# A @ y2 of a graph layer from seven products of blocks instead of a full product

## The chip, the cores and the metric

The kernel runs on one core of one Trainium2 chip. The metric is the time of one execution on the device in microseconds (us); of several executions the median is taken. The engines of the core are named as the profile names them: PE (TensorE, matrix multiplication; PEld is its loading of weights), DVE (VectorE), ACT (ScalarE), POOL (GpSimd) and SP (SyncE, which here only issues transfers).

## The reference

x is 1250 x 1024, the graph has 41250 edges (with both directions and loops), all weights are 1024 x 1024, all in float32:

```python
def _sage_sum(h, src, dst, Ws, Wn, b):
    h_neigh = jax.ops.segment_sum(h[src], dst, num_segments=N_NODES)
    return h @ Ws + h_neigh @ Wn + b

h = jnp.maximum(_layernorm(x, axis=-1), 0.0)
h = _sage_sum(h, src, dst, Ws1, Wn1, b1)
h = _sage_sum(h, src, dst, Ws2, Wn2, b2)
return x + h
```

The sum over neighbours is a product with A, the 1250 x 1250 matrix of edge counts, so h_neigh @ Wn = A @ (h @ Wn).

## The kernel before

Stage 1 builds A from the edges with one-hot matmuls, normalizes x, and computes y1 = h @ Wn1. Stage 2 computes h1 = h @ Ws1 + A @ y1 + b1, transposed, one feature tile of 128 after the other. Stage 3 is what the change is about.

All of stage 3 has the matrices cut into 2 x 2 blocks. Rows of nodes are padded to 1280, so a block of nodes is 640 = MB (5) tiles of 128 rows; a block of features is 512 = HALF, or KB (4) tiles of 128. First come s2 = h1 @ Ws2 and y2 = h1 @ Wn2, each from seven products of blocks in place of eight (Strassen). The tables say how: LEFT[m] and RIGHT[m] name the one block or the two (with their sum or difference) that product m multiplies, TARGETS[m] the output blocks to which it is added or from which it is subtracted. SEQUENCE is the order of the 14 products ("s" for s2, "y" for y2); the last is ("y", 6). A product runs over KB steps, in each over MB tiles of rows; a number is split into a rounded part (HI) and the remainder (LO), and a tile of a step takes three matmuls of 512 columns. The left sums are made by POOL (L650, from h1T), rounded by ACT (L826) and split by DVE (L1028: sum minus rounded part, both in SBUF). The right sums come ready from DRAM. PE works in eight PSUM banks in turn; `evict` (L1009) adds a finished tile on DVE from its bank to each target, in SBUF. s2 holds x and b2 already when the products begin to be added. The evictions of a product are written down in DVE's program inside the third step of the next product.

Then comes out = s2 + A @ y2, with A whole. y2 is split by column halves: `y2_split_high` on ACT (L805) and `y2_split_low` on DVE (L1015). For every half and every tile t of 128 rows, `neighbours` (L1199) runs 10 source tiles x 2 parts of y2 = 20 matmuls into one bank (L1208); A's entries are small whole numbers and need no split. DVE adds the bank to s2 (L1047, after `dve.wait_ge(tile_done, g + 1)`), and SP writes each tile to the output (L532).

Each engine runs its own program in order and waits on semaphores, so an instruction that waits holds up all behind it on its engine. `bank_free(g)` makes PE wait before the first matmul in a bank until what the bank held is evicted.

Of the kernel before, what the change touches and what calls it, by code (L numbers as in the profile page):

```python
# [4 lines left out]
F32 = mybir.dt.float32  # L5
# [55 lines left out]
            ("y", 2), ("s", 2), ("y", 3), ("y", 6))  # L61
STEPS = len(SEQUENCE) * KB
PARTIALS = len(SEQUENCE) * MB
BANKS2 = (6, 7, 0, 1, 2, 3, 4, 5)
# [47 lines left out]

def evictions():


    seen = set()
    for p, (what, m) in enumerate(SEQUENCE):
# [12 lines left out]
def writes_of(what, row, col, i):  # L130

    seen, found = {"ACT": 0, "DVE": 0}, []
    for p, j, r, c, _, engine in evictions():
        seen[engine] += 1
        if (SEQUENCE[p][0], r, c, j) == (what, row, col, i):
            found.append((p, engine, seen[engine]))
# [96 lines left out]
def gnn_kernel(nc, x, src, dst, ws1, wn1, b1, ws2, wn2, b2, out):  # L233
# [5 lines left out]
    with ctx:  # L239
# [77 lines left out]
        y2_low = at("y2_low", [P, NT, D], F32R, NT * D * 4)  # L317
        y2_high = at("y2_high", [P, 2, NT, HALF], F32R, R0)
# [54 lines left out]
        y2_hi = sem("y2_hi"); y2_lo = sem("y2_lo"); out_ready = sem("out_ready"); out_saved = sem("out_saved")  # L373
# [13 lines left out]
        def wait_step(engine, n):  # L387
# [4 lines left out]
            else:  # L392
                engine.wait_ge(step_done, p * (KB - 1) + k + 1)

# [4 lines left out]
        def _(sp):  # L399
# [128 lines left out]
            for half in range(2):  # L528
                for t in range(NT):
                    r = rows_of(t)  # L530
                    sp.wait_ge(out_ready, half * NT + t + 1)
                    sp.dma_start(out[t * P:t * P + r, half * HALF:(half + 1) * HALF],  # L532
                                 s2[:r, t, half * HALF:(half + 1) * HALF]).then_inc(out_saved, 16)
# [4 lines left out]
        def _(pool):  # L538
# [105 lines left out]
            for n in range(STEPS):  # L644
# [6 lines left out]
                if 3 * KB <= n < 3 * KB + NT:  # L651
                    add_bias(n - 3 * KB)


        @block.scalar
        def _(act):
# [143 lines left out]
            def y2_split_high(half, t):  # L800

                r = rows_of(t)
                act.wait_ge(left_summed, left_sums(10 if half == 0 else len(SEQUENCE) - 1))
                act.wait_ge(dve_evicted, writes_of("y", t // MB, half, t % MB)[-1][2])
                nc.scalar.activation(y2_high[:r, 1 - half, t, :], y2[:r, t, half * HALF:(half + 1) * HALF],  # L805
                                     ACT.Copy).then_inc(y2_hi, 1)

# [3 lines left out]
            for n in range(STEPS):  # L811
# [20 lines left out]
                if 11 * KB <= n < 11 * KB + NT:  # L832
                    y2_split_high(0, n - 11 * KB)
            evict(len(SEQUENCE) - 1, range(MB))
            for t in range(NT):
                y2_split_high(1, t)
# [3 lines left out]
        def _(dve):  # L840
# [152 lines left out]
            done = [0]  # L993

            def evict(p, tiles):
                what = SEQUENCE[p][0]
                for q, i, row, col, op, engine in evictions():
                    if q == p and i in tiles and engine == "DVE":
# [11 lines left out]
                        done[0] += 1  # L1010

            def y2_split_low(half, t):
                r, c = rows_of(t), slice(half * HALF, (half + 1) * HALF)
                dve.wait_ge(y2_hi, half * NT + t + 1)
                nc.vector.tensor_tensor(y2_low[:r, t, c], y2[:r, t, c], y2_high[:r, 1 - half, t, :].bitcast(F32),  # L1015
                                        ALU.subtract).then_inc(y2_lo, 1)

            for n in range(STEPS):
# [17 lines left out]
                if 11 * KB <= n < 11 * KB + NT:  # L1036
                    y2_split_low(0, n - 11 * KB)
            evict(len(SEQUENCE) - 1, range(MB))
            for t in range(NT):
                y2_split_low(1, t)  # L1040
            for half in range(2):
                for t in range(NT):
                    g, r = PARTIALS + half * NT + t, rows_of(t)
                    c = s2[:r, t, half * HALF:(half + 1) * HALF]
                    dve.wait_ge(dve_evicted, done[0])
                    dve.wait_ge(tile_done, g + 1)  # L1046
                    nc.vector.tensor_tensor(c, c, PS[:r, BANKS2[g % 8], :], ALU.add).then_inc(out_ready, 1)  # L1047


        @block.tensor  # L1050
        def _(pe):
# [116 lines left out]
            def bank_free(g):  # L1168
# [4 lines left out]
                elif g - 8 < PARTIALS:  # L1173
                    pe.wait_ge(act_evicted, evicted("ACT", g - 8))
                    pe.wait_ge(dve_evicted, evicted("DVE", g - 8))
                else:
                    pe.wait_ge(out_ready, g - 8 - PARTIALS + 1)

# [20 lines left out]
            def neighbours(half, t, dt):  # L1199
                g = PARTIALS + half * NT + t  # L1200
                bank_free(g)
                for s in range(NT):
                    r = rows_of(s)
                    if t == 0:
                        pe.wait_ge(y2_lo, half * NT + s + 1)
                    for part in (HI, LO):
                        y = y2_high[:r, 1 - half, s, :] if part == HI else y2_low[:r, s, half * HALF:(half + 1) * HALF]
                        ins = nc.tensor.matmul(PS[:rows_of(t), BANKS2[g % 8], :],  # L1208
                                               AT[:r, s, t * P:t * P + rows_of(t)].bitcast(dt), y.bitcast(dt),
                                               start=s == 0 and part == HI, stop=s == NT - 1 and part == LO)  # L1210
                ins.then_inc(tile_done, 1)

            for want, dt in ((0, F32R), (1, F32)):
                with pe.If(redo == want):
# [4 lines left out]
                    for half in range(2):  # L1219
                        for t in range(NT):  # L1220
# [19 lines left out]
```

## Time and profile before

| | |
|---|---|
| median of 3 executions | 660.74 us (658.27 to 661.71) |
| the profiled execution, its own time | 660.24 us |
| its span, first to last instruction | 658.4 us |
| PE busy in the span | 637.4 us (97%) |
| DVE / ACT / POOL busy | 280.3 / 175.7 / 212.4 us |
| PE from the start of s2 and y2 to their end | 372.7 to 563.1 us |
| PE in A @ y2 | 563.1 to 655.0 us |

The profile is of one execution. Matmuls overlap, so the record of one (389 ns) is longer than the time that PE moves on in; that is the length of a stretch divided by its matmuls. On other engines too a record is a little longer than the distance between two instructions in a queue.

### The profile page before, as it was taken

Reading aid. Unit: us, or ns where it says so; the run is one execution under the profiler, and the core shown is the slowest. Engines: PE = TensorE matmul, PEld = TensorE weight load, DVE = VectorE, ACT = ScalarE, POOL = GpSimd, SP = SyncE. Lnnn points to the kernel's source line nnn. Section 1 sums busy time; section 2 is a strip of 40 time slices with the busy share of each in tenths; the row PEclk is TensorE's granted clock in tenths of the full one; section 3 lists DMA queues with packets and bytes.
Section 4 is the critical chain, followed back from the end, with each engine's and each line's share of the span. In section 5 each row is a group of like instructions: output and inputs, shape, how many; then the busy total and the mean of one; then the engine's idle time right before and its main releaser. Section 6 shows DMA issues by size and latency. Waiting matters only on the chain.

```text
span 658.4 us, 8500 instructions
## 1 busy us (share of the span) xinstructions
PE 637.4 (97%) x3280; PEld 555.4 (84%) x3280; DVE 280.3 (43%) x386; ACT 175.7 (27%) x292; POOL 212.4 (32%) x201
## 2 busy tenths in 40 slices
PE   3799999999899999999999999999999999999997
PEld 2688778887799999999999988888888888887885
DVE  2653799783111211120122383325287987611111
ACT  5444343222213313323233121311334433100000
POOL 5432335000247656775680157103214013000000
PEclk9899999999999999999999999999999999999999
DMA  8622330001446766566755766455422243011111
GB/s 276 216 40 56 85 112 33 33 33 62 137 135 196 258 222 232 199 223 202 259 216 176 246 223 231 157 159 160 127 81 69 76 160 96 33 54 59 61 48 62
DMA packets 62724, 90.61 MB, mean 138 GB/s; under 512 B 16545, under 2 KB 34987, under 8 KB 62678
## 3 DMA queue, kind: packets, MB, share of 16 engines
q1 hardware_dynamic: 42342, 76.08, 34.6%
q10 hardware_dynamic: 20336, 13.91, 6.8%
q8 instruction: 30, 0.49, 0.3%
q14 instruction: 16, 0.13, 0.1%
HBM read 58.49 MB, written 31.48 MB: 137 GB/s over the span
## 4 chain that ended last, share of the span: by engine, by line
PE 62%; DMA 1%; DVE 0%; ACT 0%; POOL 0%; issue 0%; SPq 0%; DVEq 0%
PE PS L1192 29%; PE PS L1208 14%; PE PS L1155 10%; PE PS L1163 9%; DMA quarters<-ws_in 1%; DVE W_st L979 0%; POOL prep_sum L617 0%; ACT W_st L728 0%; DVE s L1047 0%; ACT prep L779 0%; SPq L487 0%; DVEq L1046 0%
## 5 line engine op out<-in xcount | busy, mean ns | idle before, releaser
L1192 PE MATMUL PS<-right,left 128*128 128x512 f32 x840 | 190.6, 389 | 0.0
L1192 PEld LDWEIGHTS PS<-right,left 128*128 128x128 f32 x840 | 157.8, 188 | 32.6
L1067 PE MATMUL PS<-W,HT 128*128 128x512 f32 (+1 forms) x480 | 123.0, 406 | 2.5 <-issue 2.4
L1155 PE MATMUL PS<-HT,W_st 128*128 128x416 f32 (+1 forms) x576 | 110.4, 352 | 2.4 <-issue 1.7
L1155 PEld LDWEIGHTS PS<-HT,W_st 128*128 128x128 f32 x576 | 107.9, 188 | 4.0 <-issue 3.1
L1067 PEld LDWEIGHTS PS<-W,HT 128*128 128x128 f32 (+1 forms) x480 | 87.8, 190 | 22.0 <-issue 2.8
L1163 PE MATMUL PS<-AT,y_st 128*128 128x416 f32 (+2 forms) x480 | 92.1, 351 | 0.0
L1163 PEld LDWEIGHTS PS<-AT,y_st 128*128 128x128 f32 (+1 forms) x480 | 90.0, 188 | 0.7
L650 POOL TENSOR_TENSOR left_sum<-h1T 128x640 f32<-128x640 f32 x24 | 41.9, 1746 | 149.9 <-PE PS L1192 120.0
L617 POOL TENSOR_TENSOR prep_sum<-quarters 128x512 f32<-128x512 f32 x40 | 51.6, 1293 | 102.8 <-PE PS L1067 62.8
L1208 PE MATMUL PS<-y_high,AT 128*128 128x512 f32 (+1 forms) x200 | 78.4, 392 | 0.0
L1208 PE MATMUL PS<-y_low,AT 128*128 128x512 f32 (+1 forms) x200 | 78.4, 392 | 0.0
L622 POOL TENSOR_TENSOR prep<-prep_sum,prep 128x512 fp32r<-128x512 f32 x40 | 60.7, 1520 | 25.9 <-ACT prep L779 25.9
L979 DVE TENSOR_TENSOR W_st<-W_st_raw,W_st 128x1024 fp32r<-128x1024 f32 x8 | 14.4, 1798 | 85.2 <-ACT W_st L728 85.2
L1208 PEld LDWEIGHTS PS<-y_low,AT 128*128 128x128 f32 (+1 forms) x200 | 37.2, 186 | 8.8
L1047 DVE TENSOR_TENSOR s<-s,PS 128x512 f32<-128x512 f32 (+1 forms) x20 | 13.7, 687 | 72.0 <-PE PS L1208 72.0
L1208 PEld LDWEIGHTS PS<-y_high,AT 128*128 128x128 f32 (+1 forms) x200 | 37.1, 185 | 8.7
L982 DVE TENSOR_TENSOR y_st<-y_st_raw,y_st 128x1152 fp32r<-128x1152 f32 x8 | 10.9, 1358 | 77.7 <-ACT y_st L765 77.7
L779 ACT ACTIVATE prep<-prep_sum 128x512 fp32r<-128x512 f32 x40 | 23.6, 624 | 64.8 <-POOL prep_sum L617 35.7
L1009 DVE TENSOR_TENSOR s<-s,PS 128x512 f32<-128x512 f32 (+1 forms) x60 | 37.2, 681 | 6.5 <-PE PS L1192 4.5
L924 DVE TENSOR_TENSOR hot_n<-iota_n,pair_key 128x1600 f16<-128x1600 f16 x40 | 39.4, 985 | 0.0
L922 DVE TENSOR_TENSOR hot_m<-iota_m,pair_m 128x1280 f16<-128x1280 f16 x40 | 33.0, 826 | 9.3 <-PE PS L1059 9.2
(79 smaller groups left out, 452.1 us busy)
## 6 DMA issues: line engine op xcount, KB each, us to landing
sums_dram<-prep SPq DMA_DIRECT2D x40, 512.0 KB, 2.9
right<-sums_dram SPq DMA_DIRECT2D x40, 512.0 KB, 3.5
y_dram<-y_out ACTq DMA_DIRECT2D x18, 256.0 KB, 2.1
y_st_raw<-y_dram ACTq DMA_DIRECT2D x8, 576.0 KB
s<-x_in SPq DMA_DIRECT2D x18, 256.0 KB
out<-s SPq DMA_DIRECT2D x18, 256.0 KB
W_raw<-wn_in SPq DMA_DIRECT2D x16, 256.0 KB, 4.0
xin<-x_in SPq DMA_DIRECT2D x8, 512.0 KB, 12.2
```

Of the source, the lines that this page charges most:

```text
L617: nc.gpsimd.tensor_tensor(prep_sum[:, i % PREP, LO, :], quarters[:, QUARTERS.index(a), :], quarters[:, QUARTERS.index(b), :], op).then_inc ...
L622: nc.gpsimd.tensor_tensor(prep[:, i % PREP, LO, :], prep_sum[:, i % PREP, LO, :], prep[:, i % PREP, HI, :].bitcast(F32), ALU.subtract).the ...
L650: nc.gpsimd.tensor_tensor(left_sum[:, k, LO, :], h1_block(*a, k), h1_block(*b, k), op).then_inc(left_summed, 1)
L779: nc.scalar.activation(prep[:, i % PREP, HI, :], prep_sum[:, i % PREP, LO, :], ACT.Copy).then_inc(prep_hi, 1)
L922: nc.vector.tensor_tensor(hot_m[:, u % HOT, :, :, :], iota_m[:, :, :].unsqueeze(1).to_broadcast([P, ROW, P, 2]), pair_m[:, u, :, :].unsque ...
L924: nc.vector.tensor_tensor(hot_n[:, u % HOT, :, :, :], iota_n[:, :, :].unsqueeze(1).to_broadcast([P, ROW, NCOL, 2]), pair_key[:, u, :, :].u ...
L1009: nc.vector.tensor_tensor(c, c, PS[:r, BANKS2[g % 8], :], op).then_inc(dve_evicted, 1)
L1067: ins = nc.tensor.matmul(PS[:r, bank, :], HT[:, a, k, t * P:t * P + r], W[:, k, b, :], start=first and m == 0, stop=last and m == 2)
L1155: ins = nc.tensor.matmul(PS[:, banks[c], 0:w_], W_st[:, a, k, :], HT[:, b, k, o_:o_ + w_], start=k == 0 and m == 0, stop=False)
L1163: ins = nc.tensor.matmul(PS[:, banks[c], 0:w_], y_st[:r, part, s, :].bitcast(dt), AT[:r, s, o_:o_ + w_].bitcast(dt), start=False, stop=s = ...
L1192: ins = nc.tensor.matmul(PS[:, BANKS2[g % 8], :], left[:, k, a, i * P:(i + 1) * P], right[:, KB - 1 - k, b, :], start=k == 0 and j == 0, s ...
L1208: ins = nc.tensor.matmul(PS[:rows_of(t), BANKS2[g % 8], :], AT[:r, s, t * P:t * P + rows_of(t)].bitcast(dt), y.bitcast(dt), start=s == 0 a ...
```

## The change

A @ y2 is now also made from seven products of blocks, in the order NEIGHBOURS = (2, 4, 5, 3, 1, 7, 6) of the same tables, with A's blocks on the left (640 x 640, MB steps of 128) and y2's on the right. Every product is added by DVE's `evict` to the one or two blocks of s2 that TARGETS names. A product has MB steps x MB tiles x 2 parts of y2 = 50 matmuls; the seventh runs tile by tile instead of step by step.

- Left: where LEFT has two blocks (products 2, 5, 1, 7, 6), POOL adds or subtracts them, one 128 x 640 slice per step, into a stage of 4 slots (`a_left_sum`), and SP copies each slice by a transfer into a ring of 8 (`a_left`). 25 sums, 25 transfers.
- Right: where RIGHT has two blocks (products 4, 3, 1, 7, 6), POOL sums a 128 x 512 slice of y2 for the step (`a_right_sum_of`), 25 sums. Every step's slice, sum or single block, is rounded by ACT and split by DVE, 35 times each, into a ring of 5 slots, one per step. A slot is free when PE has finished the same step of the product before.
- The rings lie in the room of h1T. `y2_split_high`, `y2_split_low` and the separate final addition are gone. The output tiles are written when their last eviction is done.

The core of the diff (`wait_a_step(engine, q)` waits until PE has finished step q of this stage):

```diff
+            def a_left_sum(li):
+                q = a_left_steps()[li]
+                a, b, op = LEFT[NEIGHBOURS[q // MB]]
+                if li >= ASTAGE:
+                    pool.wait_ge(a_left_in[(li - ASTAGE) % ALEFT], 16 * ((li - ASTAGE) // ALEFT + 1))
+                nc.gpsimd.tensor_tensor(a_stage[:, li % ASTAGE, :], a_block(*a, q % MB), a_block(*b, q % MB), op).then_inc(a_left_summed, 1)
+            def a_right_sum_of(q):
+                (ra, ca), (rb, cb), op = RIGHT[NEIGHBOURS[q // MB]]
+                wait_a_step(pool, q - MB)
+                pool.wait_ge(dve_evicted, max(written("y", ra, ca, q % MB), written("y", rb, cb, q % MB)))
+                nc.gpsimd.tensor_tensor(a_right_sum[:, q % MB, LO, :], result("y", ra, ca, q % MB), result("y", rb, cb, q % MB),
+                                        op).then_inc(a_right_summed, 1)
+            lefts = 0
+            for q in range(ASTEPS):
+                while lefts < len(a_left_steps()) and (a_left_steps()[lefts] <= q + MB or lefts < MB):
+                    a_left_sum(lefts)
+                    lefts += 1
+                if a_right_is_sum(q // MB):
+                    a_right_sum_of(q)
...
-            for t in range(NT):
-                y2_split_high(1, t)
+            for q in range(ASTEPS):
+                m = NEIGHBOURS[q // MB]
+                if a_right_is_sum(q // MB):
+                    act.wait_ge(a_right_summed, a_right_sums(q) + 1)
+                    whole = a_right_sum[:, q % MB, LO, :]
...
+                nc.scalar.activation(a_right[:, q % MB, HI, :], whole, ACT.Copy).then_inc(a_right_hi, 1)
...
+            last = len(SEQUENCE) - 1
+            for q in range(ASTEPS):
+                p, k = divmod(q, MB)
+                if k == MB - 2 and p:
+                    evict(last + p, range(2))
+                dve.wait_ge(a_right_hi, q + 1)
...
+                nc.vector.tensor_tensor(a_right[:, k, LO, :], whole, a_right[:, k, HI, :].bitcast(F32),
+                                        ALU.subtract).then_inc(a_right_lo, 1)
+                if k == MB - 2 and p:
+                    evict(last + p, range(2, MB))
+                if q == MB - 1:
+                    evict(last, range(MB))
+            evict(last + len(NEIGHBOURS), range(MB))
...
+                def two_products(k, i):
                     for part in (HI, LO):
...
+                        ins = nc.tensor.matmul(PS[:, BANKS2[(PARTIALS + p * MB + i) % 8], :], a_factor(p, k, i).bitcast(dt),
+                                               a_right[:, k, part, :].bitcast(dt),
+                                               start=k == 0 and part == HI, stop=k == MB - 1 and part == LO)
```

In what follows a line of the instruction order is the line of the kernel, the operation, what it writes and reads, its shape, and xN for N in a row.

PE, from the end of the block products to the end of the program. `right`, `left` are the factors of s2 and y2; before, the last rows of 400 that alternate:

```order
L1208 MATMUL PS<-y_high,AT 98x512
L1208 MATMUL PS<-y_low,AT 98x512
L1208 MATMUL PS<-y_high,AT 98x512
L1208 MATMUL PS<-y_low,AT 98x512
L1214 UNCONDITIONAL_BRANCH
```

and now:

```order
1882 L1258 MATMUL PS<-right,left 128x512 x840
1883 L1282 MATMUL PS<-a_right,a_left 128x512 x50
1884 L1282 MATMUL PS<-a_right,AT 128x512 x50
1885 L1282 MATMUL PS<-a_right,a_left 128x512 x50
1886 L1282 MATMUL PS<-a_right,AT 128x512 x50
1887 L1282 MATMUL PS<-a_right,a_left 128x512 x150
1888 L1308 UNCONDITIONAL_BRANCH
```

Seven products of 50 matmuls stand where 400 matmuls stood; five of them take sums of A's blocks from the ring.

POOL, after its last sum of h1's blocks (16 of them in a row close its work before; then its program ends):

```order
162 L640 TENSOR_TENSOR s_92<-s_92,b_sb 128x512 x9
163 L640 TENSOR_TENSOR s_92<-s_92,b_sb 98x512
164 L650 TENSOR_TENSOR left_sum<-h1T 128x640 x16
165 L239 UNCONDITIONAL_BRANCH
```

and now (`a_stage<-AT` is an A sum, `a_right_sum<-y_93` a sum of y2's blocks; this pattern goes on to row 203):

```order
164 L699 TENSOR_TENSOR left_sum<-h1T 128x640 x16
165 L708 TENSOR_TENSOR a_stage<-AT 128x640 x6
166 L714 TENSOR_TENSOR a_right_sum<-y_93 128x512
167 L708 TENSOR_TENSOR a_stage<-AT 128x640
168 L714 TENSOR_TENSOR a_right_sum<-y_93 128x512
169 L708 TENSOR_TENSOR a_stage<-AT 128x640
170 L714 TENSOR_TENSOR a_right_sum<-y_93 128x512
171 L708 TENSOR_TENSOR a_stage<-AT 128x640
```

50 instructions are added behind the end of its program; from the sixth on, each A sum stands directly ahead of a sum of y2's blocks.

DVE, from the middle of the last block product to the end of the program, before (`y_93` is y2, `s_92` is s2; L1009 evicts a bank, L1015 splits y2, L1047 is the final addition):

```order
830 L1009 TENSOR_TENSOR y_93<-y_93,PS 128x512 x6
831 L1028 TENSOR_TENSOR left<-left_sum,left 128x640
832 L1009 TENSOR_TENSOR y_93<-y_93,PS 128x512 x5
833 L1015 TENSOR_TENSOR y_low<-y_93,y_high 128x512 x9
834 L1015 TENSOR_TENSOR y_low<-y_93,y_high 98x512
835 L1047 TENSOR_TENSOR s_92<-s_92,PS 128x512 x9
836 L1047 TENSOR_TENSOR s_92<-s_92,PS 98x512
```

and now, in the fourth to sixth product of A @ y2 (L1077 evicts, L1109 splits):

```order
833 L1109 TENSOR_TENSOR a_right<-a_right_sum,a_right 128x512 x3
834 L1077 TENSOR_TENSOR s_92<-s_92,PS 128x512 x4
835 L1109 TENSOR_TENSOR a_right<-a_right_sum,a_right 128x512
836 L1077 TENSOR_TENSOR s_92<-s_92,PS 128x512 x6
837 L1109 TENSOR_TENSOR a_right<-a_right_sum,a_right 128x512 x4
838 L1077 TENSOR_TENSOR s_92<-s_92,PS 128x512 x4
839 L1109 TENSOR_TENSOR a_right<-a_right_sum,a_right 128x512
```

Splits and evictions alternate: the first two tiles of a product (4 evictions) stand behind the splits of the next product's first three steps.

## Rows read from the trace of the kernel before

**Rows 1.** The chain that ended last: start us, us, what.

```profile
372.72 190.43 PE PS L1192 x840
563.14 91.83 PE PS L1208 x400
655.07 0.69 DVE s L1047
```

**Rows 2.** Busy time by stretch: PE, PEld, DVE, ACT, POOL, clock, DMA share, GB/s.

```profile
563.00:586.00 23.00, 23.00 (x102) 18.89 (x101) 9.71 (x16) 1.76 (x3) 0.00 (x0) 1.00 0.12 46
609.00:632.00 23.00, 23.00 (x102) 18.85 (x101) 3.44 (x5) 0.00 (x0) 0.00 (x0) 1.00 0.15 55
```

**Rows 3.** The page's groups, DVE: busy us, mean ns | idle before, releaser.

```profile
L1047 DVE TENSOR_TENSOR s<-s,PS 128x512 f32<-128x512 f32 (+1 forms) x20 | 13.7, 687 | 72.0 <-PE PS L1208 72.0
```

**Rows 4.** The instructions of L650 on POOL: ns min/median/max, first and last start.

```profile
L650 POOL TENSOR_TENSOR left_sum<-h1T x24: 1567/1593/2290, 376.3 to 549.6; 128x640 f32<-128x640 f32 x24
```

**Rows 5.** Order of time, POOL with full queue: start us, us, instruction, idle before.

```profile
262.61 1.28 POOL L617 TENSOR_TENSOR prep_sum<-quarters 128x512 f32<-128x512 f32 x1 [5.12 <-DMA quarters<-wn_in]
263.86 1.29 POOL L622 TENSOR_TENSOR prep<-prep_sum,prep 128x512 fp32r<-128x512 f32 x1
...
400.03 1.57 POOL L650 TENSOR_TENSOR left_sum<-h1T 128x640 f32<-128x640 f32 x1 [1.83 <-PE PS L1192]
401.56 13.09 POOL L640 TENSOR_TENSOR s<-s,b_sb 128x512 f32<-128x512 f32 x10
```

**Rows 6.** Order of time, DVE and POOL near the end of the block products.

```profile
542.80 0.81 DVE L1028 TENSOR_TENSOR left<-left_sum,left 128x640 fp32r<-128x640 f32 x1
542.83 2.21 POOL L650 TENSOR_TENSOR left_sum<-h1T 128x640 f32<-128x640 f32 x1 [1.83 <-PE PS L1192]
543.53 2.05 DVE L1015 TENSOR_TENSOR y_low<-y,y_high 128x512 fp32r<-128x512 f32 x1
...
545.84 0.83 DVE L1028 TENSOR_TENSOR left<-left_sum,left 128x640 fp32r<-128x640 f32 x1 [0.26 <-ACT left L826]
546.23 1.87 POOL L650 TENSOR_TENSOR left_sum<-h1T 128x640 f32<-128x640 f32 x1 [1.19 <-PE PS L1192]
```

**Rows 7.** Order of time, evictions on DVE across a POOL sum.

```profile
536.45 3.67 DVE L1009 TENSOR_TENSOR s<-s,PS 128x512 f32<-128x512 f32 x6
...
539.43 1.57 POOL L650 TENSOR_TENSOR left_sum<-h1T 128x640 f32<-128x640 f32 x1 [28.67 <-PE PS L1192]
```

**Rows 8.** The instructions of L805 on ACT and L1015 on DVE.

```profile
L805 ACT ACTIVATE y_high<-y x20: 614/616/636, 515.4 to 564.1; 128x512 fp32r<-128x512 f32 x18, 98x512 fp32r<-98x512 f32 x2
...
L1015 DVE TENSOR_TENSOR y_low<-y,y_high x20: 681/689/2059, 516.8 to 569.4; 128x512 fp32r<-128x512 f32 x18, 98x512 fp32r<-98x512 f32 x2
```

**Rows 9.** Order of time, the last matmul.

```profile
654.57 0.40 PE L1208 MATMUL PS<-y_low,AT 98*98 98x512 f32 x1
```

**Rows 10.** Order of time, PE released by DVE.

```profile
245.23 1.94 DVE L979 TENSOR_TENSOR W_st<-W_st_raw,W_st 128x1024 fp32r<-128x1024 f32 x1 [14.71 <-ACT W_st L728]
...
247.32 0.81 PE L1155 MATMUL PS<-HT,W_st 128*128 128x416 f32 x3 [0.68 <-DVE W_st L979]
```

**Rows 11.** PE's pauses near the start in order of time, and stretches as in rows 2.

```profile
13.46 2.90 PE L1067 MATMUL PS<-W,HT 128*128 128x512 f32 x6 [2.42 <-issue]
...
22.28 1.10 PE L1093 MATMUL PS<-ident,hbuf 128*128 128x128 f32 x8 [3.58 <-ACT hbuf L685]
...
15.00:20.00 5.00, 3.70 (x18) 2.71 (x16) 1.79 (x6) 2.06 (x3) 0.16 (x1) 1.00 1.03 371
20.00:25.00 5.00, 2.72 (x13) 2.34 (x14) 5.00 (x9) 2.27 (x2) 4.92 (x4) 0.82 0.88 274
25.00:30.00 5.00, 5.00 (x38) 3.80 (x37) 1.95 (x6) 1.75 (x2) 2.25 (x4) 0.84 0.42 143
```

**Rows 12.** The page's DMA issues: count, KB each, us to landing.

```profile
right<-sums_dram SPq DMA_DIRECT2D x40, 512.0 KB, 3.5
```

More of the change, by code:

```diff
@@ L110, in prepared, with a_left_is_sum, a_left_steps, a_right_is_sum @@
     return [i for i in range(NSUMS) if 1 + i * PARTS // NSUMS == part]
+def a_left_is_sum(p):
+    return len(LEFT[NEIGHBOURS[p]]) == 3
+def a_left_steps():
+    return [q for q in range(ASTEPS) if a_left_is_sum(q // MB)]
+def a_right_is_sum(p):
+    return len(RIGHT[NEIGHBOURS[p]]) == 3
+def a_right_sums(q):
+    return sum(a_right_is_sum(i // MB) for i in range(q))
 def evictions():
     seen = set()
-    for p, (what, m) in enumerate(SEQUENCE):
+    for p, (what, m) in enumerate(SEQUENCE + tuple(("s", m) for m in NEIGHBOURS)):
         blocks = [(what, row, col) for row, col, _ in TARGETS[m]]
@@ L134, in writes_of @@
         seen[engine] += 1
-        if (SEQUENCE[p][0], r, c, j) == (what, row, col, i):
+        if (SEQUENCE[p][0] if p < len(SEQUENCE) else "s", r, c, j) == (what, row, col, i):
             found.append((p, engine, seen[engine]))
@@ L831, in _ @@
                     evict(p - 1, range(2, MB))
[L832 to L835, printed above, removed]
-                y2_split_high(1, t)
+            for q in range(ASTEPS):
[3 more added lines that the diff above has]
+                    whole = a_right_sum[:, q % MB, LO, :]
+                else:
+                    (row, col), = RIGHT[m]
+                    wait_a_step(act, q - MB)
+                    act.wait_ge(dve_evicted, written("y", row, col, q % MB))
+                    whole = result("y", row, col, q % MB)
+                nc.scalar.activation(a_right[:, q % MB, HI, :], whole, ACT.Copy).then_inc(a_right_hi, 1)
         @block.vector
@@ L1035, in _ @@
                     evict(p - 1, range(2, MB))
[L1036 to L1047, printed above, removed]
+            last = len(SEQUENCE) - 1
[4 more added lines that the diff above has]
+                dve.wait_ge(a_right_hi, q + 1)
+                if a_right_is_sum(p):
+                    whole = a_right_sum[:, k, LO, :]
+                else:
+                    (row, col), = RIGHT[NEIGHBOURS[p]]
+                    whole = result("y", row, col, k)
+                nc.vector.tensor_tensor(a_right[:, k, LO, :], whole, a_right[:, k, HI, :].bitcast(F32),
[5 more added lines that the diff above has]
+            evict(last + len(NEIGHBOURS), range(MB))
         @block.tensor
@@ L1197, in partial_products, with a_factor @@
                         ins.then_inc(step_done, 1)
[L1199 to L1205, printed above, removed]
-                    for part in (HI, LO):
[L1207 to L1211, printed above, removed]
+            def a_factor(p, k, i):
+                if a_left_is_sum(p):
+                    return a_left[:, a_left_steps().index(p * MB + k) % ALEFT, i * P:(i + 1) * P]
+                (row, col), = LEFT[NEIGHBOURS[p]]
+                return AT[:, col * MB + k, (row * MB + i) * P:(row * MB + i + 1) * P]
@@ L1218, in _ @@
                         partial_products(p)
[L1219 to L1221 removed]
+                    for p in range(len(NEIGHBOURS)):
+                        neighbour_products(p, dt)
 def kernel(x, src, dst, L0_gnn_Ws1, L0_gnn_Wn1, L0_gnn_b1, L0_gnn_Ws2, L0_gnn_Wn2, L0_gnn_b2):
```

86 lines of the change are left out of this document (61 added, 25 removed).

## The prediction

> **What bounds the kernel now.** I read the chain of waits first. From 372.72 us to the end it names only the matrix engine: 840 matmuls of the block products in 190.43 us, then 400 matmuls of A @ y2 in 91.83 us, then one addition of 0.69 us that starts 655.07 us into the span [rows 1]. That is 0.2296 us for a matmul of A @ y2 (91.83 / 400) and 0.2267 us before it (190.43 / 840). The table by stage says how alone the engine is there: in 609 to 632 us PE is busy 23.00 of 23.00 us, DVE 3.44, ACT and POOL nothing; only in the first stretch, 563 to 586, is DVE still splitting, 9.71 us [rows 2]. DVE's 20 additions of this stage waited 72.0 us in all for PE [rows 3]. So PE sets the end, each matmul taken away is worth 0.2296 us, and the question is what the emptied engines can carry.
>
> **What goes.** 400 matmuls become 7 products x 5 steps x 5 tiles x 2 parts = 350. Matmuls keep their shape, so 50 x 0.2296 = 11.5 us go if PE never waits. (At 0.2267 us it would be 12.5; I keep 0.2296, since these products too take one part of y2 after the other.) Also gone are the 20 splits of y2, ten beside the last block products and ten beside the first tiles. They lay under a busy PE and are worth nothing, except that DVE reaches the new work sooner.
>
> **What comes.** A product now lasts only 25 x 2 x 0.2296 = 11.5 us, a step 2.3 us. Against that:
> DVE, in each of the five products with two targets: 10 evictions and 5 splits at 0.61 us each (3.67 us for six in a row [rows 7], splits alike) = 9.2 us. It fits.
> ACT: 5 roundings of 0.62 us [rows 8] = 3.1 us. It fits.
> POOL: a sum of A blocks has the form of the sums of h1 blocks, 128x640, of 1567 to 1593 ns when undisturbed [rows 4]; behind one that started at 400.03 the next began at 401.56, so 1.53 us in a queue. A 128x512 sum of y2 blocks has the form of those that start at 262.61 and 263.86, 1.25 us apart [rows 5]. The ring of A sums is filled a product ahead, one A sum before each y2 sum, so while the fourth, fifth and sixth product run, POOL owes 5 x (1.53 + 1.25) = 13.9 us for each 11.5 us of PE.
> The 25 transfers of an A sum are 320 KB; the nearest row lands 512 KB in 3.5 us [rows 12]. They have 8 places and run most of a product ahead: nothing.
>
> **POOL and DVE exclude each other here.** A split on DVE that began at 543.53 lasted 2.05 us instead of the usual 0.69 [rows 8]. POOL's sum of 542.83 ended at 545.04, the split 0.54 us later. In turn that sum took 2.21 us, not 1.57: DVE's split of 542.80 ended at 543.61, and 545.04 - 1.57 is 543.47. The pair at 545.84 and 546.23 reads the same (POOL 1.87) [rows 6]. So either engine waits for the other; a split between two queued POOL sums holds POOL up by 0.54 - 0.14 + 0.04 (end of a record against its neighbour) = about 0.45 us. Evictions do not: six ran from 536.45 in 3.67 us across a POOL sum of 1.57 [rows 7]; one operand of theirs is in PSUM. The Trainium skill, SBUF — State Buffer, "Who interferes with whom", says why: a DVE instruction with two SBUF inputs and a GpSimd instruction that reads SBUF exclude each other wholly, one with a single SBUF input does not. The trace agrees in both halves. By that rule the 35 splits and 50 sums of the new stage can never overlap.
>
> **Who waits for it.** On DVE's queue a product's first two tiles are evicted only after three splits of the next product. PE needs the first of these banks at that product's fourth tile, 3 x 0.46 = 1.4 us after its start. So PE waits when the third split is late.
> Second product: POOL may sum y2 for k = 0 when PE has finished the first step, 565.5. Sum 1.29 to 566.8, A sum to 568.3, split 0.45, then sum, A sum, 0.45, sum: 573.2. ACT to 573.9; the next A sum holds DVE to 574.8, split 0.55, two evictions 1.2, 0.2 until PE restarts: 576.7. (The restart: a DVE result at 245.23 + 1.94 = 247.17, the matmul at 247.32 [rows 10].) PE wanted the bank at 563.0 + 11.5 + 1.4 = 575.9: it waits 0.8, and 0.75 more for the next tile (two evictions and a restart, less a tile's work). The third product needs no y2 sums: no wait.
> From the fourth product's first y2 sum POOL is never idle. It may start when the third product's first step is done: 563.0 + 11 x 2.296 + 1.6 waited + 0.2 = 590.1. Up to the sixth product's third y2 sum it owes 13 x 1.25 + 12 x 1.53 + about 12 x 0.45 = 40.0 us: 630.1. ACT to 630.8, the A sum in progress to 631.7, split 0.55, two evictions, restart: 633.7. That is when PE gets its fourth bank of the sixth product, and all waits before it are contained in it: a product in which POOL makes ten sums takes 5 x (1.53 + 1.25 + 0.45) = 16.1 us, so PE waits 4.6 in the fifth and as much in the sixth, and by difference 2.0 in the fourth. Then 1.2 us to the next tile, whose 21 pairs of matmuls to the product's end take 21 x 0.459 = 9.6: 644.5. The last product runs tile by tile and wants all five splits within its first 5 pairs. The last y2 sum can start only now; at 645.3 behind a split, to 646.6, ACT 647.2, split 647.9, restart: PE waits at its fifth pair (due 646.4) till 648.1, 1.7 us. 21 pairs are left, 9.6 us: 657.7. The final addition starts 0.24 us after the last matmul's slot (654.57 + 0.23 against 655.07 [rows 9]) plus 0.69: 658.6.
> Before, it ended at 655.76. The sum is +2.9 us: 11.5 saved, 14.4 waited (1.6, 2.0, 4.6, 4.6, 1.7). What follows, the landing of a last tile of the same size, is unchanged. On the profiled execution's 660.24 that gives 663.1 us, which stands 0.4% above the median of 660.74.
>
> **Rivals.**
> (a) PE is fed throughout: 660.24 - 11.5 = 648.8. For it: PE did not wait from 372.72 us to its end, and POOL, ACT stood idle. Against: POOL's 13.9 us to PE's 11.5 needs no subtle mechanism.
> (b) The queue of POOL binds, but a split costs it nothing (because the sums of A run further ahead, or splits fall into gaps). Then the fifth and sixth product wait 13.9 - 11.5 = 2.4 each and the last one 1.3 (1.7 less the 0.4 behind a split): 11.5 - 6.1 = 5.4 us gained, 654.8. Against it stand the four records of [rows 6].
> (c) Slower, plainly: POOL's sums on A are 5% longer, or splits hold POOL up by 0.55 each. From 590.1 on POOL is the chain, so 34.6 us x 5% = 1.7, or 12 x 0.1 = 1.2, goes fully into the end; with both, and with the second product's wait and the last product's grown alike, some 4 us: 667.1. It decides as soon as POOL has no idle left, which by the sum is the whole time from 590.1.
> (d) The waits lower PE's clock. After 3.58 us without matmuls, at 22.28, the granted clock of 20 to 25 us is 0.82, that of 15 to 20 us 1.00: part of it at 1.2 instead of 2.4 GHz. After the pause of 2.42 us before 13.46 it stayed at 1.00 [rows 11]. The waits of the fifth and sixth product are 3.9 us in one piece. Such a pause cost (1 - 0.82) x 5 + (1 - 0.84) x 5 = 1.7 us of PE's work there; but in these products PE has 4.6 us of waiting in which it makes that up, so only a loss near the end counts: +1.7 twice at most, 666.5. The Trainium skill, TensorE: Matmul & The Clock Gate, "Why this matters for your kernels", holds that a pause between bursts of matmuls can send the engine back to its lower clock; it speaks against this change.
>
> **How the numbers follow.** The forecast 0.70, with its own range 661 to 666: whether a split meets a POOL sum at its start or its end moves a wait by up to 1.5 us, and several of these add. (a) 0.04, (b) 0.10, (c) 0.10, (d) 0.06. A measurement of this kernel tells 0.5% from no change: under 657.4 is faster, over 664.0 slower. The forecast gives slower 0.28 and the same 0.40 of its 0.70, with a little to faster; (a) and (b) are faster, (c) and (d) slower. Together: faster 0.15, same 0.42, slower 0.43. For 8 in 10 the range leaves out (a) and most of (b), and takes in the bounds of (c) and (d): 656.5 to 667.5.
>
> **What would show it.** In the profile after: 350 matmuls of the new line, PE with idle time before them of some 14 us, ended by DVE's evictions, two waits near 4 us in the fifth and sixth product; POOL busy nearly without a gap from 590 to 645 us; splits whose mean is well over 0.69 us and A sums over 1.57. If the splits are at 0.69 us and the POOL sums at 1.6, (b) is right; if PE shows no idle, (a); if the clock of 615 to 650 us is under 1.00, part of (d). I am wrong if POOL's sums are shorter than the rows of before, or if PE's waits are ended by ACT or a transfer.

## The result, and the profile after

Six executions of each kernel, on the same chips in turn: 666.4 us median (664.0 to 667.6) against 660.2 (658.3 to 661.7). The ratio is 1.0089 with a 95% interval of 1.0069 to 1.0109. The change makes the kernel slower by 0.9%. The prediction was 663.1, slower by 0.4%: its direction was right and its range held the time, but the slowdown came out more than twice as large. The profiled execution took 667.12 us, of which 665.3 are the span. Here and below, executions more than 1.5% above the fastest of their kernel are left out of every comparison.

What answers to [rows 1 and 3], in order of time on PE (start us, us, instruction, idle before it and who ended it), from the last block product to the end:

```profile
559.72 2.88 PE L1258 MATMUL PS<-right,left 128*128 128x512 f32 x12
562.44 11.96 PE L1282 MATMUL PS<-a_right,a_left 128*128 128x512 f32 x50
574.24 1.52 PE L1282 MATMUL PS<-a_right,AT 128*128 128x512 f32 x6
576.55 0.70 PE L1282 MATMUL PS<-a_right,AT 128*128 128x512 f32 x2 [0.78 <-DVE s L1077]
577.74 9.78 PE L1282 MATMUL PS<-a_right,AT 128*128 128x512 f32 x42 [0.49 <-DVE s L1077]
587.36 11.50 PE L1282 MATMUL PS<-a_right,a_left 128*128 128x512 f32 x50
598.69 1.52 PE L1282 MATMUL PS<-a_right,AT 128*128 128x512 f32 x6
601.49 0.70 PE L1282 MATMUL PS<-a_right,AT 128*128 128x512 f32 x2 [1.27 <-DVE s L1077]
602.69 11.42 PE L1282 MATMUL PS<-a_right,AT 128*128 128x512 f32 x42 [0.50 <-DVE s L1077]
613.95 1.52 PE L1282 MATMUL PS<-a_right,a_left 128*128 128x512 f32 x6
617.57 0.70 PE L1282 MATMUL PS<-a_right,a_left 128*128 128x512 f32 x2 [2.10 <-DVE s L1077]
618.77 11.16 PE L1282 MATMUL PS<-a_right,a_left 128*128 128x512 f32 x48 [0.49 <-DVE s L1077]
633.65 0.70 PE L1282 MATMUL PS<-a_right,a_left 128*128 128x512 f32 x2 [3.72 <-DVE s L1077]
634.84 12.52 PE L1282 MATMUL PS<-a_right,a_left 128*128 128x512 f32 x48 [0.49 <-DVE s L1077]
648.07 0.70 PE L1282 MATMUL PS<-a_right,a_left 128*128 128x512 f32 x2 [0.71 <-DVE a_right L1109]
650.46 11.39 PE L1282 MATMUL PS<-a_right,a_left 128*128 128x512 f32 x42 [1.69 <-DVE a_right L1109]
```

Where PE had no idle there are now ten waits. Eight stand before the fourth and fifth tile of the second, fourth, fifth and sixth product and are ended by an eviction (L1077); two stand in the seventh product and are ended by a split (L1109). A record of a matmul (0.39 us) is longer than its slot (0.227), so each wait is 0.16 us longer than the idle shown. Together PE waited 13.8 us, where the prediction had 14.4. The waits are thus not what was missing in the sum.

The groups of POOL and DVE in the page after (busy us, mean ns | idle before):

```profile
L714 POOL TENSOR_TENSOR a_right_sum<-y 128x512 f32<-128x512 f32 x25 | 40.4, 1619 | 15.2 <-PE PS L1282 15.1
L708 POOL TENSOR_TENSOR a_stage<-AT 128x640 f32<-128x640 f32 x25 | 42.1, 1693 | 0.0
...
L1109 DVE TENSOR_TENSOR a_right<-a_right_sum,a_right 128x512 fp32r<-128x512 f32 x25 | 30.1, 1208 | 17.0 <-ACT a_right L906 16.4
```

A sum of y2 blocks takes 1.62 us where 1.29 was the undisturbed record [rows 5], a split 1.21 where 0.69 was the median [rows 8]. That is what the exclusion of [rows 6] would do; the experiments test it.

And by stretch, as in [rows 2] (PE, PEld, DVE, ACT, POOL, granted clock, DMA share, GB/s):

```profile
600.00:617.00 17.00, 13.70 (x51) 10.40 (x50) 13.15 (x18) 3.16 (x5) 17.00 (x11) 0.90 0.25 96
617.00:633.00 16.00, 11.86 (x50) 9.23 (x50) 12.17 (x16) 3.16 (x5) 16.00 (x11) 1.00 0.27 102
633.00:640.00 7.00, 5.86 (x19) 4.49 (x20) 7.00 (x12) 1.90 (x3) 5.62 (x5) 0.76 0.14 50
640.00:650.00 10.00, 8.07 (x35) 6.06 (x33) 7.43 (x10) 2.53 (x4) 5.59 (x4) 1.00 0.98 360
650.00:662.00 12.00, 11.39 (x42) 8.93 (x42) 3.12 (x6) 0.00 (x0) 0.00 (x0) 0.86 0.37 138
```

POOL is busy 17.00 of 17.00 and 16.00 of 16.00 us: it is the bound there. The clock is below 1.00 in three stretches, each behind a wait; behind the wait of 2.10 us at 617.57 it stayed at 1.00. The 42 matmuls from 577.74 took 9.78 us; those from 602.69 took 11.42, those from 650.46 11.39.

### The profile page after: what moved, and what is told of

Same layout as the page of the kernel before. It is cut to its first block and busy times, and to the rows that moved or that the text cites. A ratio compares the mean times of both kernels' runs of the same rounds, so it can differ in the third digit from the quotient of the medians.

```text
span 665.3 us, 8676 instructions
## 1 busy us (share of the span) xinstructions
PE 632.3 (95%) x3230; PEld 548.4 (82%) x3230; DVE 328.5 (49%) x441; ACT 186.0 (28%) x307; POOL 296.8 (45%) x251
## 5 line engine op out<-in xcount | busy, mean ns | idle before, releaser
L1135 PEld LDWEIGHTS PS<-W,HT 128*128 128x128 f32 (+1 forms) x480 | 86.4, 187 | 23.8 <-issue 2.8
L1077 DVE TENSOR_TENSOR s<-s,PS 128x512 f32<-128x512 f32 (+1 forms) x120 | 74.4, 677 | 17.5 <-PE PS L1282 7.9
L1282 PE MATMUL PS<-a_right,a_left 128*128 128x512 f32 x250 | 62.1, 406 | 9.3 <-DVE s L1077 6.8
L1282 PEld LDWEIGHTS PS<-a_right,a_left 128*128 128x128 f32 x250 | 48.5, 196 | 22.4 <-issue 12.3
L714 POOL TENSOR_TENSOR a_right_sum<-y 128x512 f32<-128x512 f32 x25 | 40.4, 1619 | 15.2 <-PE PS L1282 15.1
L708 POOL TENSOR_TENSOR a_stage<-AT 128x640 f32<-128x640 f32 x25 | 42.1, 1693 | 0.0
L1109 DVE TENSOR_TENSOR a_right<-a_right_sum,a_right 128x512 fp32r<-128x512 f32 x25 | 30.1, 1208 | 17.0 <-ACT a_right L906 16.4
```

The costliest lines, as they stand in the source:

```text
L708: nc.gpsimd.tensor_tensor(a_stage[:, li % ASTAGE, :], a_block(*a, q % MB), a_block(*b, q % MB), op).then_inc(a_left_summed, 1)
L714: nc.gpsimd.tensor_tensor(a_right_sum[:, q % MB, LO, :], result("y", ra, ca, q % MB), result("y", rb, cb, q % MB), op).then_inc(a_right_su ...
L1077: nc.vector.tensor_tensor(c, c, PS[:r, BANKS2[g % 8], :], op).then_inc(dve_evicted, 1)
L1135: ins = nc.tensor.matmul(PS[:r, bank, :], HT[:, a, k, t * P:t * P + r], W[:, k, b, :], start=first and m == 0, stop=last and m == 2)
L1282: ins = nc.tensor.matmul(PS[:, BANKS2[(PARTIALS + p * MB + i) % 8], :], a_factor(p, k, i).bitcast(dt), a_right[:, k, part, :].bitcast(dt), ...
```

## Experiments

Three questions were open. Is it POOL's queue that binds, or only the place of the evictions in DVE's queue? Does the exclusion of POOL and DVE cost what the sum says, or is it DVE's added work? And what does the clock cost? A time below is a median; a ratio, with its 95% interval, is to the kernel before, run in turn on the same chip.

**Evictions ahead of the third split.** One condition in DVE's program:

```diff
-                if k == MB - 2 and p:
+                if k == MB - 3 and p:
                     evict(last + p, range(2))
                 dve.wait_ge(a_right_hi, q + 1)
```

> DVE evicts the first two tiles of a product before the third split of the next one instead of behind it. Theory POOL (from the fourth product on, POOL's queue of sums, held up further by splits, is the chain): the waits at the fourth tile shrink in the second and fourth product, but the fifth and sixth still wait some 2.7 + 0.8 us each and new waits of about 1 us appear at a product's last step; the end moves by 1 to 2 us only, 664 to 665.5 us against 666.4. Rival ORDER (the place of the evictions in DVE's queue is what costs): nearly all 10 us of waits for evictions go, about 656 us.

663.8 us, ratio 1.0049 (1.0012 to 1.0085). That is a little less than the 664 to 665.5 expected. The waits of the second and fourth product for a bank are gone, those of the fifth and sixth are not, and PE waits at last steps for splits instead:

```profile
607.15 2.57 PE L1282 MATMUL PS<-a_right,AT 128*128 128x512 f32 x10 [0.59 <-DVE a_right L1109]
609.55 1.52 PE L1282 MATMUL PS<-a_right,a_left 128*128 128x512 f32 x6
613.61 13.59 PE L1282 MATMUL PS<-a_right,a_left 128*128 128x512 f32 x50 [2.54 <-DVE s L1077]
629.68 0.70 PE L1282 MATMUL PS<-a_right,a_left 128*128 128x512 f32 x2 [2.47 <-DVE s L1077]
```

If DVE's order were the cause, 10 us would have gone; 2 to 3 went. The order passes most of POOL's lateness on, it is not its source.

**Without the sums of A's blocks.** SP's transfer takes a slice of A itself, and POOL's `a_left_sum` is not called:

```diff
-                sp.wait_ge(a_left_summed, li + 1)
-                sp.dma_start(a_left[:, li % ALEFT, :].bitcast(F32), a_stage[:, li % ASTAGE, :]).then_inc(a_left_in[li % ALEFT], 16)
+                sp.dma_start(a_left[:, li % ALEFT, :].bitcast(F32), a_block(*LEFT[NEIGHBOURS[q // MB]][0], q % MB)).then_inc(a_left_in[li % ALEFT], 16)
```

> Leaves out part of the computation: the 25 sums of A's blocks on POOL; the ring takes a slice of one block of A instead, by the same transfers. Theory POOL: POOL owes 6.2 us per product instead of 13.9, so no wait for evictions is left but one of 0.5 us in the second product, the last product still waits some 1.7 us, the last eviction ends 9.5 us earlier than in the kernel before (655.8 - 9.5 = 646.3 us into the span), about 651 us in all. Rival ORDER: POOL's sums were not the cause, waits near 4 us stay in the fifth and sixth product, 660 us or more. Theory CLOCK on top (pauses lower the granted clock): with few pauses the clock of the stretch after 563 us is 1.00 throughout.

One execution counts, of 654.7 us. The waits of 2.1 and 3.7 us in the fifth and sixth product are gone, without any change to DVE's order: 0.38 us is left in the second and in the fourth product, 0.71 and 1.69 in the seventh. So POOL's 25 sums of A blocks made the big waits. It was not as short as expected (651), because the 42 matmuls at the end still took 11.39 us, and A @ y2 began 1.7 us later in this execution, at 564.14.

**Without splits on DVE.** ACT writes a second rounded copy, DVE only evicts:

```diff
-                nc.scalar.activation(a_right[:, q % MB, HI, :], whole, ACT.Copy).then_inc(a_right_hi, 1)
+                nc.scalar.activation(a_right[:, q % MB, HI, :], whole, ACT.Copy)
+                nc.scalar.activation(a_right[:, q % MB, LO, :], whole, ACT.Copy).then_inc(a_right_lo, 1)
...
-                nc.vector.tensor_tensor(a_right[:, k, LO, :], whole, a_right[:, k, HI, :].bitcast(F32),
-                                        ALU.subtract).then_inc(a_right_lo, 1)
```

> Leaves out part of the computation: the 35 splits on DVE; ACT writes a second rounded copy where the remainder would stand (0.62 us more per step on an idle engine). POOL's 50 sums stay. Theory POOL with exclusion: without a DVE instruction that has both inputs in SBUF no POOL sum is longer than 1.30 us (y2 blocks) or 1.60 us (A blocks), against means of 1.62 and 1.69 now; the product with ten sums takes 13.9 us, so waits of about 2.4 us remain in the fifth and sixth; the end is near 655 us (the price of exclusion alone some 8 to 10 us of the 666.4). Rival QUEUE ONLY (exclusion costs nothing, POOL's own work does it): the waits stay near 4 us and the end within 2 us of 666.4.

650.5 us, ratio 0.9816 (0.9703 to 0.9928, from two executions). All 50 sums are still there, and now last 1.31 and 1.59 us (from 563 us on; the A sums of the changed kernel took 1.63 us there):

```profile
L714 POOL TENSOR_TENSOR a_right_sum<-y 128x512 f32<-128x512 f32 x25 | 32.4, 1309 | 12.9 <-PE PS L1275 12.9
L708 POOL TENSOR_TENSOR a_stage<-AT 128x640 f32<-128x640 f32 x19 | 30.2, 1592 | 0.0
```

It gained more than the 655 us expected. PE's longest idle is 0.55 us, since not only the exclusion but also DVE's own work on the splits is gone. That mixes two causes, and the next kernel goes some way to part them.

**One SBUF input in place of two.** DVE keeps an instruction at the place of each split, with its waits. It reads one input in place of two, and it writes one column in place of 512; ACT writes a second rounded copy, as in the last kernel:

```diff
-                nc.scalar.activation(a_right[:, q % MB, HI, :], whole, ACT.Copy).then_inc(a_right_hi, 1)
+                nc.scalar.activation(a_right[:, q % MB, HI, :], whole, ACT.Copy)
+                nc.scalar.activation(a_right[:, q % MB, LO, :], whole, ACT.Copy).then_inc(a_right_hi, 1)
...
-                nc.vector.tensor_tensor(a_right[:, k, LO, :], whole, a_right[:, k, HI, :].bitcast(F32),
-                                        ALU.subtract).then_inc(a_right_lo, 1)
+                if q:
+                    dve.wait_ge(a_right_lo, q)
+                nc.vector.reduce_sum(unused[:, 1:2], a_right[:, k, HI, :].bitcast(F32), axis=mybir.AxisListType.X).then_inc(a_right_lo, 1)
```

> Leaves out part of the computation: in place of each of the 35 splits DVE sums up the rounded slice (one input in SBUF, about as long as a split), at the same place in its queue and with the same waits; ACT writes a second rounded copy where the remainder would stand, 0.55 us more before DVE may start. So DVE's queue and work stay, and only the second SBUF input goes. Theory EXCLUSION: POOL's sums take 1.3 and 1.6 us, DVE's replacements about 0.7 us and none is stretched; PE's waits in the fifth and sixth product fall from 2.6 and 4.2 us to about 2.5 to 3 each (POOL's 13.9 us against 11.3), those in the second and fourth to under 0.5; some 8 us less than the changed kernel's 666.4, 656 to 659 us. Rival DVE WORK (what the run without any splits gained came from DVE's shorter queue): the waits stay and the time is within 2 us of 666.4.

657.1 us, ratio 0.9936 (0.9905 to 0.9967). The time is in the expected range. The replacement takes as long as an undisturbed split, and neither engine's instructions are stretched:

```profile
L714 POOL TENSOR_TENSOR a_right_sum<-y 128x512 f32<-128x512 f32 x25 | 32.5, 1303 | 17.3 <-PE PS L1284 17.3
L708 POOL TENSOR_TENSOR a_stage<-AT 128x640 f32<-128x640 f32 x19 | 30.1, 1587 | 0.0
...
L1112 DVE TENSOR_REDUCE unused<-a_right 128x1 f32<-128x512 f32 x30 | 20.5, 682 | 23.3 <-ACT a_right L907 22.9
```

So the exclusion costs the changed kernel 1.0089 - 0.9936 = 1.5% of 660 us, 10 us (some 8 to 12 by the two intervals), although ACT's second copy made the chain 0.55 us longer here. It isn't all waiting: by the two profiles PE waited 13.8 us in the one and 6.1 in the other, and about a third of the difference is matmuls at less than full pace, most of it the lower clock behind the longer waits. That it is the input and not the 511 columns less to write wasn't tried by itself; but evictions write 512 columns to SBUF as well, and with one input there they stretched nobody [rows 7]. The 6 to 8 us from here to the kernel without splits (ACT's second copy is in both) are what DVE's own step costs: its 0.68 us behind ACT's in the chain and the evictions' wait behind it. Some of them are again the clock, since the fifth product lost 1.8 us by it here; they are not parted further.

**Waits filled with matmuls.** PE repeats a tile's first matmul, which opens the sum anew each time, so the result is the same:

```diff
+                            if k == 0 and i == 2:
+                                repeat_first(k, i, {1: 3, 3: 5, 4: 9, 5: 15}.get(p, 0))
...
+                            if k == 0 and i == 0:
+                                repeat_first(k, i, 10)
```

> PE repeats the first matmul of a tile (3, 5, 9 and 15 times in the second, fourth, fifth and sixth product, 10 times at the start of the seventh), with the same result, so that most of each wait is filled with matmuls; all else is as in the changed kernel. Theory CLOCK: the pauses are what lowers the granted clock (0.87, 0.73 and 0.89 in stretches after the waits of 1.3, 3.7 and 1.7 us); with them filled it stays at 1.00 after 563 us, the 42 matmuls at the end take 9.6 us instead of 11.4, and the time is 663 to 664 us, 2 to 3 below the changed kernel, though 42 matmuls more are issued. Rival: the clock falls anyway, or the filling delays the chain: 666.4 or more, up to 668.

664.9 us, ratio 1.0071 (1.0030 to 1.0111), which can't be told from 1.0089 and is above the 663 to 664 expected. In the profiled execution of 663.6 us the matmuls at the end kept their pace, as did the 46 of the sixth product:

```profile
633.44 10.59 PE L1287 MATMUL PS<-a_right,a_left 128*128 128x512 f32 x46
...
648.49 9.77 PE L1287 MATMUL PS<-a_right,a_left 128*128 128x512 f32 x42 [0.38 <-DVE a_right L1109]
```

The fifth product's wait wasn't filled whole: an idle of 1.78 us was left, and the 46 matmuls behind it took 12.32 us:

```profile
616.69 0.70 PE L1287 MATMUL PS<-a_right,a_left 128*128 128x512 f32 x2 [1.78 <-DVE s L1077]
617.89 12.32 PE L1287 MATMUL PS<-a_right,a_left 128*128 128x512 f32 x46 [0.49 <-DVE s L1077]
```

The mean granted clock of its ten executions is 0.994 to 0.997, of the changed kernel's six 0.990 to 0.994. So the lower clock goes with the pauses; that filling them gains time is not shown.

**The seventh product step by step.**

```diff
-                if p == len(NEIGHBOURS) - 1:
+                if p == len(NEIGHBOURS):
```

> The seventh product runs step by step like the others instead of tile by tile; nothing else changes. Theory: the 0.7 and 1.7 us that PE waits at the fourth and fifth pair of this product, and the 1.8 us that its last 42 matmuls lose to the lower clock behind these waits, go; against that its five tiles all end within the last 2.3 us, so DVE ends about 1.3 us later behind PE. The waits of the second to sixth product stay. Sum: about 663.5 us against 666.4. Rival: the last splits are late anyway and PE waits for them at the fourth and fifth step, or the five evictions and writes at the end cost more than 3 us: 666 us or more.

664.3 us, ratio 1.0061 (1.0037 to 1.0085), 2 us under the changed kernel where 3 were expected; the intervals overlap and don't part them. In the profile the two waits of the seventh product are gone, and no wait for its splits took their place.

**The sums of A's blocks early.** POOL makes them during the products of s2 and y2, one or two per step where `new_left` asks nothing of it, and SP parks them in DRAM:

```diff
+                for li in a_sums_at(n - 1):
+                    sp.wait_ge(a_left_summed, li + 1)
+                    sp.dma_start(a_sums_dram[li, :, :], a_stage[:, li % ASTAGE, :]).then_inc(a_stored[li % ASTAGE], 16)
...
-                sp.dma_start(a_left[:, li % ALEFT, :].bitcast(F32), a_stage[:, li % ASTAGE, :]).then_inc(a_left_in[li % ALEFT], 16)
+                sp.dma_start(a_left[:, li % ALEFT, :].bitcast(F32), a_sums_dram[li, :, :]).then_inc(a_left_in[li % ALEFT], 16)
...
             for n in range(STEPS):
...
+                for li in a_sums_at(n):
+                    a_left_sum(li)
```

> POOL makes the 25 sums of A's blocks during the products of s2 and y2, from the sixth on, where it waited for PE; SP writes them to DRAM and loads them back into the ring of eight during the products of A @ y2. All else as in the changed kernel. Theory POOL: the same end as with the A sums left out, whose one undisturbed run was 654.7 us: waits of about 0.4 us in the second and fourth product, 0.7 and 1.7 in the seventh with 1.8 us of lower clock behind them; 652 to 655 us. Rival: the 25 sums now collide with the splits of h1 and with POOL's left sums, and PE waits before 563 us, or the loads come late: 656 us or more.

654.0 us, ratio 0.9908 (0.9874 to 0.9943): nothing of the computation is left out, and it is faster than the kernel before. PE's record of 372 to 563 us is as full as ever; the sums hid there. The waits that remain are those of the run without the sums.

> The A sums early (as in the run before) and the seventh product step by step. Theory: the two effects add, since each takes away its own waits: 2.4 us of waits and 1.8 us of lower clock less, 1.3 us of evictions at the end more, so some 2.5 us under the kernel with early sums alone: 650 to 652 us. Rival: they don't add, 653 us or more.

With both of the last two edits: 650.8 us, ratio 0.9847 (0.9792 to 0.9903). That is the 650 to 652 expected of two effects that add; the interval of four executions is too wide to show more.

> The A sums early, the seventh product step by step, and the first two tiles of a product evicted before the third split of the next. Theory: PE has no wait left after 563 us and the clock stays at 1.00; 350 matmuls in 79.4 us (at 0.2267 us) from 563.0, then about 2.3 us until the last eviction is done: 644.7 us into the span, 649.3 us in all (it ended at 655.8 with 660.2 in all before). Rival: the earlier evictions delay the third split so that PE waits there instead: 651 us or more.

With the earlier evictions too: 649.1 us, ratio 0.9817 (0.9778 to 0.9856), where 649.3 was expected. After 562.61 PE has no wait left; its last three products are one record:

```profile
562.61 11.50 PE L1293 MATMUL PS<-a_right,a_left 128*128 128x512 f32 x50
573.95 11.49 PE L1293 MATMUL PS<-a_right,AT 128*128 128x512 f32 x50
585.28 11.50 PE L1293 MATMUL PS<-a_right,a_left 128*128 128x512 f32 x50
596.61 11.50 PE L1293 MATMUL PS<-a_right,AT 128*128 128x512 f32 x50
607.95 34.16 PE L1293 MATMUL PS<-a_right,a_left 128*128 128x512 f32 x150
```

This is what the 50 matmuls less are worth: 11 us, as rival (a) had it for a PE that is always fed.

**The clock once more.** The kernel with early sums, with and without 10 repeats at the start of the seventh product, side by side on one chip:

> The kernel with early A sums, and PE repeats the first matmul of the seventh product 10 times with the same result (2.3 us), so that it has no pause before the fourth and fifth pair, which waited 0.7 and 1.7 us. Theory CLOCK: the wait itself is only filled, but the last 42 matmuls take 9.6 to 9.8 us instead of 11.4, so the time is about 1.6 us below the kernel with early sums run beside it. Rival: what is slow after the wait is not the pause's doing, or the filling delays the last steps: the same time or more.

> The kernel with early A sums once more, to be compared with the filled one on the same chip: 653 to 655 us, the last 42 matmuls in 11.4 us behind the wait of 1.7 us.

653.3 us, ratio 0.9890 (0.9864 to 0.9916), against 654.2, ratio 0.9911 (0.9889 to 0.9933): 0.9 us, inside the uncertainty, so the 1.6 us expected of the filling are not shown. In the filled kernel's profile the last 42 matmuls took 9.77 us, as expected, but this was its longest execution, 659.11 us: A @ y2 began only at 570.02. The unfilled one met its time but not its 11.4 us at the end: of its two profiled executions, the first (of the earlier experiment) had the slow end and the second had not, behind the same wait:

```profile
635.19 11.41 PE L1293 MATMUL PS<-a_right,a_left 128*128 128x512 f32 x42 [1.69 <-DVE a_right L1120]
```

```profile
639.28 9.79 PE L1293 MATMUL PS<-a_right,a_left 128*128 128x512 f32 x42 [1.69 <-DVE a_right L1120]
```

So behind a wait of 1.7 us the clock falls in some executions, not in all. The twelve traces with the block products in A @ y2 give a count for the time after 560 us (two waits a tile apart are one here). Sixteen waits had an idle of 1.27 us or more in one piece. Behind eleven of them the next 42 or more matmuls took 1.5 to 2.8 us longer than at full pace, behind five they kept it. Behind the waits with less idle in one piece (up to 0.81 us) no such loss followed, and none came without a wait. What decides among the sixteen stays open.

## Why the prediction was right in its way and wrong in its size

The mechanism was right: POOL's queue of sums, made longer by the splits, is the chain, and PE waits for DVE's evictions, 13.8 us in all. Its signs came too, with splits and y2 sums well over their undisturbed times (of the A sums only the mean, 1.69 us, not the median of 1.57). Up to 633.65 us the sum was right, mostly to 0.1 us. POOL's chain was to begin at 590.1 and reach the end of the sixth product's third y2 sum at 630.1; it began at 589.87 and reached it at 628.53 + 1.73 = 630.26:

```profile
589.87 1.30 POOL L714 TENSOR_TENSOR a_right_sum<-y 128x512 f32<-128x512 f32 x1 [8.77 <-PE PS L1282]
...
628.53 1.73 POOL L714 TENSOR_TENSOR a_right_sum<-y 128x512 f32<-128x512 f32 x1
```

PE was to get its bank at 633.7; it did at 633.65. The waits, each with its 0.16 us: second product 0.78 + 0.49 + 0.33 = 1.6 (predicted 1.6), fourth 2.1 (2.0), sixth 4.5 (4.6). The fifth waited 2.9 and not 4.6, because the 42 matmuls before it took 1.7 us longer at the lower clock: as the prediction said of rival (d), PE made that up out of its waiting, POOL's chain did not move.

The step that failed is the last one of the sum, from PE's restart at 633.7 to the end: 24.9 us predicted, 662.63 - 633.65 = 29.0 measured. It let every matmul run at full pace and so put the clock, its own rival (d), at nothing; and it had the last split too early. The 4.1 us have three parts.

- Clock, sixth product (with the first six matmuls of the seventh): 48 in 12.52 us, where 48 slots and a record's tail are 48 x 0.2267 + 0.16 = 11.04. 1.5 us, and the last y2 sum, which waits for this product's last step, started at 646.09 and not at 645.3.
- Clock, seventh product: 42 matmuls in 11.39, where 42 x 0.2267 + 0.16 = 9.68. 1.7 us.
- The last split. The prediction had it at 647.9 and PE waiting 1.7 us. PE waited 0.71 + 1.69 + 0.33 = 2.7. The fourth split was late as well, and the term left out the other splits and evictions at this place:

```profile
646.09 1.29 POOL L714 TENSOR_TENSOR a_right_sum<-y 128x512 f32<-128x512 f32 x1 [0.69 <-PE PS L1282]
```

```profile
646.09 1.83 DVE L1109 TENSOR_TENSOR a_right<-a_right_sum,a_right 128x512 fp32r<-128x512 f32 x1 [0.53 <-ACT a_right L906]
647.85 1.87 DVE L1077 TENSOR_TENSOR s<-s,PS 128x512 f32<-128x512 f32 x3
649.64 0.68 DVE L1109 TENSOR_TENSOR a_right<-a_right_sum,a_right 128x512 fp32r<-128x512 f32 x1
```

POOL's last sum and DVE's fourth split start together; the split loses and ends at 647.92. Three evictions are queued behind it, so the fifth split, rounded by ACT at 648.04, starts at 649.64. The sum had the exclusion for POOL, but for DVE only where it held up an eviction; here it held up a split through the evictions. That DVE's work "fits", 9.2 us in a product, had been added up with splits of 0.61 us; with them at 1.21 DVE was busy 7.00 of 7.00 us from 633 to 640.

A smaller error went the other way and hid: a matmul of A @ y2 had been costed at 0.2296 us, the pace of the stage before. In the kernel with no waits 50 take 11.34 us (562.61 to 573.95), 0.2268 each. 350 of them are 1.0 us less than the prediction's. In the changed kernel the first product, 562.44 to 574.24, was 0.5 us over that pace. Its record is 11.95 to 11.99 us long in the four traces in which DVE's first five splits meet POOL's first A sums, and 11.49 to 11.50 in the eight in which they don't. The changed kernel's trace shows what fits this, though it was not tested:

```profile
555.47 7.80 DVE L1109 TENSOR_TENSOR a_right<-y,a_right 128x512 fp32r<-128x512 f32 x5 [0.70 <-ACT a_right L906]
563.18 3.06 DVE L1077 TENSOR_TENSOR y<-y,PS 128x512 f32<-128x512 f32 x5
```

The five splits took 7.80 us, and the evictions of the last block product, which free banks for this one, began only 0.7 us after it had. In the kernel with no waits the splits took 3.10 us and the evictions began 2.5 us ahead of the product.

Of the rivals, (a) and (b) are refuted: PE waits, and the exclusion costs 10 us. (c) is not what happened either, though it has a time near the measured one: POOL's chain took 40.4 us where the sum had 40.0. (d), the clock, had been given 0.06 and a price of +1.7 us twice, 666.5. It came, at about that price (1.5 + 1.7 us), in the profiled execution, on top of the forecast; with the 1.0 us of the last split this makes the 4.1. The forecast's own range, 661 to 666, missed the median by 0.4 us; the wide one held it since it took in the bounds of (c) and (d). What had been read right in [rows 11] was that 3.58 us of pause lower the clock; what had been read too much into them was that 2.42 us don't. The trace after shows the drop behind 1.27 + 0.50 and 0.71 + 1.69 us. The chance was too small since one row with a pause that left the clock alone was taken as a bound.

The median of 666.4 lies 0.7 us under the profiled 667.12. How the other five executions share their time between waits and clock is not on record.

## What to carry over

A product saved on the busiest engine pays only if the engines that prepare its operands have the time for one product, not for one kernel: count each helper's work against the new, shorter product, and add what two helpers that exclude each other cost, on both of them. Work that depends on nothing recent (here the sums of A) belongs where its engine waits anyway, even by way of DRAM: moved there, with two changes of order that together gave another 0.9%, the same change gave 0.9817 instead of 1.0089. And a wait for a helper can have a second price on the bound engine, the clock behind it. While a helper's chain sets the end, PE makes this up out of its next wait; at the end of the chain it is paid in full.

## What was not expected of the hardware

The granted clock fell behind pauses as short as 1.27 + 0.50 us (42 matmuls in 11.42 us instead of 9.78) and 0.71 + 1.69 us, and did not behind 2.10 + 0.49 us (48 in 11.16) in the same execution. Behind the same 1.69 us one execution of the same kernel had 11.41 us and another 9.79.

The exclusion of POOL and DVE was expected, and went with the second SBUF input: with one input at the same place a y2 sum took 1.30 us, with two 1.62. The Trainium skill, SBUF — State Buffer, "Who interferes with whom", states this rule; these runs agree.
